# A sparse mixture's first products rotate through four banks late in the loop, with rows transposed three tiles ahead, gating four steps behind and outputs six behind

## What is computed

```python
logits = jnp.einsum('bsd,de->bse', x, Wg)
top_vals, top_idx = jax.lax.top_k(logits, TOP_K)          # 2 of 8
probs = jax.nn.softmax(top_vals, axis=-1)
for e in range(E):
    u = jnp.einsum('bsd,dh->bsh', x, W1[e])               # 128 -> 256
    v = jnp.einsum('bsd,dh->bsh', x, W2[e])
    h = u * jax.nn.sigmoid(u) * v
    y = jnp.einsum('bsh,hd->bsd', h, W3[e])               # 256 -> 128
    out = out + y * weights[..., e][..., None]
x = x + jnp.tanh(g_ffn[1]) * out
```

## Time and profile before

| | us |
|---|---|
| median of 3 runs | 926.17 |
| lowest, highest | 923.63, 931.97 |
| profiled execution, its own time | 930.39 |
| its span, first to last instruction | 928.6 |
| mean granted TensorE clock | 0.933 |

### The profile page before, as it was taken

One profiled execution on the slowest core, in us unless ns is written; L12 is line 12 of the kernel. 1 busy time (PEld: TensorE's weight loads), 2 busy tenths in 40 slices (PEclk: granted clock), 3 DMA queues, 4 the chain that ended last, 5 costly groups with the idle time before them and its releaser, 6 DMA issues. The chain is left out here.

```text
span 928.6 us, 26325 instructions
## 1 busy us (share of the span) xinstructions
PE 793.4 (85%) x8408; PEld 610.8 (66%) x8408; DVE 720.4 (78%) x3041; ACT 571.9 (62%) x1209; POOL 466.9 (50%) x504
## 2 busy tenths in 40 slices
PE   4999999999999599999998898865678888888870
PEld 2566666666666356677775676765577887888860
DVE  3989899889898769899999988644465666668864
ACT  3777777777776456887887766443334555555530
POOL 3653454445444011376676765646555554555550
PEclk9999999999999879989999989877779999999995
DMA  9001001000100200011111111311122322245628
GB/s 242 30 23 41 20 20 37 22 20 20 39 1 2 59 1 10 13 50 45 46 45 39 53 44 35 88 49 58 58 67 73 96 79 69 78 125 163 178 81 277
DMA packets 62211, 57.95 MB, mean 62 GB/s; under 512 B 10320, under 2 KB 52099, under 8 KB 62115
## 3 DMA queue, kind: packets, MB, share of 16 engines
q1 hardware_dynamic: 44547, 34.25, 13.2%
q0 software_dynamic: 8640, 17.84, 5.7%
q10 hardware_dynamic: 8928, 4.70, 1.8%
HBM read 32.74 MB, written 24.02 MB: 61 GB/s over the span
## 5 line engine op out<-in xcount | busy, mean ns | idle before, releaser
L1113 POOL DMA_INDIRECT contributions<-v_heads,d_token x142 | 136.6, 962 | 120.4 <-DVE v_heads L1301 76.2
L1741 PE MATMUL bc_bank<-d_xT,d_w 128*128 128x128 f32 x1136 | 161.9, 288 | 39.7 <-DVE b_hidden L1290 17.1
L1741 PEld LDWEIGHTS bc_bank<-d_xT,d_w 128*128 128x128 f32 x1136 | 145.7, 201 | 46.8 <-DVE d_xT L1285 35.1
L1105 POOL DMA_INDIRECT sorted_rows<-r_send,r_slots x128 | 126.8, 990 | 50.2 <-issue 34.6
L1510 ACT ACTIVATE b_hidden<-bc_bank 128x256 f32<-128x256 f32 x142 | 54.4, 383 | 154.4 <-PE bc_bank L1741 121.1
L1285 DVE COPY d_xT<-bc_bank 128x128 f32<-128x128 f32 x142 | 40.8, 287 | 94.3 <-PE bc_bank L1760 66.3
L432 POOL TENSOR_SCALAR a_k_heads<-a_kT,first 128x512 f32<-128x512 f32 x60 | 93.2, 1570 | 0.8 <-ACT a_kT L483 0.8
L1517 ACT COPY d_w<-w 128x512 f32 x142 | 86.9, 612 | 2.2
L507 ACT ACTIVATE a_probs<-a_scores 128x1024 f32<-128x1024 f32 x64 | 65.6, 1025 | 29.4 <-PE a_scores L607 29.3
L350 DVE TENSOR_REDUCE a_neg_max<-a_scores 128x16 f32<-128x1024 f32 x64 | 78.1, 1220 | 6.8 <-PE a_scores L597 5.3
L514 ACT COPY a_probsT<-a_probsT_bank 128x512 f32<-128x512 f32 x128 | 74.7, 584 | 11.7 <-PE a_probsT_bank L624 11.1
(11 more groups left out here) (215 smaller groups left out, 1884.8 us busy)
## 6 DMA issues: line engine op xcount, KB each, us to landing
d_rows<-sorted_rows SPq DMA_DIRECT2D x142, 65.0 KB
X<-in_x SPq DMA_DIRECT2D x16, 256.0 KB, 3.0
b_hidden<-contributions SPq DMA_DIRECT2D x8, 512.0 KB
b_weighted<-contributions SPq DMA_DIRECT2D x8, 512.0 KB
out_x<-X ACTq DMA_DIRECT2D x16, 256.0 KB
ctxT<-in_ctx_T SPq DMA_DIRECT2D x16, 192.0 KB, 2.9
c_ctxT<-in_ctx_T SPq DMA_DIRECT2D x16, 192.0 KB
contributions<-v_heads,d_token POOLq DMA_INDIRECT x142
```

What stands on the lines that cost most here:

```text
L1105: pool.indirect_dma_start(dispatch.rows, bass.IndirectOffsetOnAxis(ap=slots[n % 2][:, k, j:j + 1], axis=0), send[n % 2][k][:, j, :], None) ...
L1113: pool.indirect_dma_start(dispatch.contributions, bass.IndirectOffsetOnAxis(ap=token[:, t % KEEP:t % KEEP + 1], axis=0), shares[t % KEEP], ...
L1741: last = pe.matmul(uv[m % 2][:, bass.ts(i, P)], w12[m % 3][:, bass.ts(i, P)], xT[m % 4][:], start=True, stop=True)
```

## The change

It changes how far behind each other the parts of a tile run, and how many banks the first products use.

| | before | after |
|---|---|---|
| first products and Silu of tile m | step m+2 | step m+3 |
| gating of tile m | step m+2 | step m+4 |
| second products and share of tile w | step w+4 | step w+6 |
| banks of first products | bc_bank0, bc_bank1 | the same below tile 20, then bc_bank0, bc_bank1 and both halves of bc_pair in turn |
| first products wait for gating of | tile m-2 | tile m-2 below tile 22, then tile m-4 |
| Silu slots | 2 | 4 |

The tiles 22 and 23 are the first ones in bc_pair; they wait for the last attention work in it. The steps run to 147 instead of 145, since the outputs of the last tiles come six steps behind.

```diff
-    HIDDEN, OUT = 2, 4
+    HIDDEN, GATED, OUT, FOUR = 3, 4, 6, 20
...
-    silu = tails[0:2]
-    d_hidden = [b.rearrange("p (k n) -> p k n", k=KH) for b in tails[2:6]]
+    silu = tails[0:4]
+    d_hidden = [b.rearrange("p (k n) -> p k n", k=KH) for b in tails[4:8]]
...
-    uv, y_bank = bank[0:2], (bank[5], bank[2])
+    y_bank = bank[5], bank[2]
+
+    def uv(m):
+        return (bank[0][:], bank[1][:], pair[:, 0], pair[:, 1])[m % 2 if m < FOUR else m % 4]
...
-                m = t - HIDDEN
+                m = t - GATED
                 if 0 <= m < DTILES:
                     dve.wait_ge(silu_done, m + 1)
-                    dve.tensor_tensor(d_hidden[m % 4].rearrange("p k n -> p (k n)"), silu[m % 2],
-                                      uv[m % 2][:, KH * P:2 * KH * P], ALU.mult).then_inc(h_ready, 1)
+                    dve.tensor_tensor(d_hidden[m % 4].rearrange("p k n -> p (k n)"), silu[m % 4],
+                                      uv(m)[:, KH * P:2 * KH * P], ALU.mult).then_inc(h_ready, 1)
...
-                    if m >= 2:
-                        act.wait_ge(h_ready, m - 1)
-                    act.activation(silu[m % 2], uv[m % 2][:, 0:KH * P], ACT.Silu).then_inc(silu_done, 1)
+                    if m >= 4:
+                        act.wait_ge(h_ready, m - 3)
+                    act.activation(silu[m % 4], uv(m)[:, 0:KH * P], ACT.Silu).then_inc(silu_done, 1)
...
-                    if m >= 2:
-                        pe.wait_ge(h_ready, m - 1)
+                    if m < 2:
+                        pe.wait_ge(k_ready if m == 0 else weighted_ready[0], G)
+                    elif m == FOUR + 2:
+                        pe.wait_ge(xrT_ready, G)
+                    elif m == FOUR + 3:
+                        pe.wait_ge(x1_updated, G)
                     else:
-                        pe.wait_ge(k_ready if m == 0 else weighted_ready[0], G)
+                        pe.wait_ge(h_ready, m - 1 if m < FOUR + 2 else m - 3)
```

More of the change, by code:

```diff
@@ L1735, in sparse @@
                     pe.wait_ge(w12_ready, m + 1)
-                    if m >= 2:
-                        pe.wait_ge(h_ready, m - 1)
+                    if m < 2:
[4 more added lines that the diff above has]
+                        pe.wait_ge(x1_updated, G)
                     else:
-                        pe.wait_ge(k_ready if m == 0 else weighted_ready[0], G)
+                        pe.wait_ge(h_ready, m - 1 if m < FOUR + 2 else m - 3)
                     for i in range(2 * KH):
-                        last = pe.matmul(uv[m % 2][:, bass.ts(i, P)], w12[m % 3][:, bass.ts(i, P)], xT[m % 4][:], start=True, stop=True)
+                        last = pe.matmul(uv(m)[:, bass.ts(i, P)], w12[m % 3][:, bass.ts(i, P)], xT[m % 4][:], start=True, stop=True)
                     last.then_inc(hidden_mm, 1)
```

## The result

| | before | after |
|---|---|---|
| median, us | 929.07 (4 runs) | 947.37 (4 runs) |
| range | 923.63 to 932.4 | 944.92 to 955.14 |
| profiled execution, its span | 928.6 | 943.1 |
| mean granted clock | 0.933 | 0.933 |

The changed kernel takes 1.0225 of the time of before, 95% interval 1.0178 to 1.0271: it is 1.8 to 2.7% slower. 913 us was predicted, in a range of 897 to 932; the result lies above the range, and the change goes the other way.

What follows compares the result with a forecast made beforehand. It took TensorE and the vector engine, waiting for each other in a ring with late TensorE signals, as the bound. Terms -17.4 - 6.9 + 10 + 1 = -13.3 us turned 926.2 into 913 us, range 897 to 932.

Steps and rivals of the forecast that it cites:

- The ring, and its tolerances of 0.45 us before and 1.34 after: TensorE and vector engine wait for each other; a signal late by up to 0.45 us, then 1.34, costs nothing.
- At the mean wait of 0.9, nothing would be left: Steps 25 to 107: at TensorE's mean gating wait of about 0.9 us, the new tolerance leaves no loss.
- the choice of 1.58 us: Steps 25 to 107: step taken as 1.58 us, between 1.47 without waiting and 1.79 now; gain 17.4 us.
- The late stretch, -6.9 us: Steps 108 to 140: 1.64 us per step instead of 1.85, with a floor of 1.54; gain 6.9 us, ends 0 and 10.
- The start, +10 us (4 to 25): First 25 steps, two banks only: the ring becomes serial, 2.50 us per step instead of 1.45; costs 10 us.
- steps 6 to 11: Part of the start, mixed with TensorE's last attention work: six serial steps at 2.50 us, 15.0 instead of 12.97; +2.0.
- The scatter behind share 11: Part of the start: routing group 15's scatter on GpSimd comes 11.4 us behind step 14 instead of 7.4; +4.0.
- the steps of the two holds: Start, 637 to 654 and 664 to 681: TensorE gets one step less far (4.0 us), two shares fewer (2.5); +3.0.
- The tail, +1 us (0 to 2.5): End of the mixture: two steps more, with second products alone; costs 1 us.
- The second one: Rival: lags use up the new tolerance; steady step 1.75 us, early +13, tail +2, 936 us; chance 0.22.
- The first rival: Rival: signal lags don't grow; steps of 1.48 and 1.56 us, about 899 us in all; chance 0.15.
- The signs it named: Prediction wrong if steady step stays above 1.70 us or falls below 1.50, or step 25 comes under 3 or over 20 later.

Runs made afterwards that it cites:

- e9: Changed kernel with shares from tile 12 on written by SyncE's queue as whole tiles, row places left out; 901.2 us, 0.9683 of the kernel before, late signals in set.
- e14: Changed kernel with four short GpSimd copies behind each share's DMA from tile 12 on; 944.9 us, 1.0197 of the kernel before, in a set with late signals.
- e15: Kernel before with shares from tile 12 on written by SyncE as whole tiles, row places left out; 881.1 us, 0.9521 of before, late signals in set.
- e11: Changed kernel with gating three behind and outputs five behind; 931.2 us, 1.0038 of the kernel before, in a set with late signals.
- e6: Changed kernel, unchanged, run again in a set without late signals; 877.7 us, 1.0255 of the kernel before.
- e5: Kernel before, unchanged, run again for a trace in a set without late signals; 855.1 us.
- e12: Kernel of e9 with two GpSimd multiplications per share from tile 12 on in place of the DMAs; 907.3 us, 0.9786 of the kernel before.
- e13: Changed kernel with shares from tile 12 on written as whole tiles from GpSimd's own queue, row places left out; 906.4 us, 0.979 of the kernel before.
- e10: Changed kernel with two short GpSimd copies behind each share's DMA from tile 12 on; 941.3 us, 1.0146 of the kernel before, late signals in set.
- e16: Kernel before with three short GpSimd copies behind each share's DMA from tile 12 on; 894.7 us, 1.0402 of before, no late signals in set.
- e17: Changed kernel with three short GpSimd copies behind each share's DMA; 900.8 us, 1.0482 of the kernel before, no late signals in set.

## Why the prediction was wrong, point by point

**The ring, and its tolerances of 0.45 us before and 1.34 after: right, or nearly, where signals are late.** Before, a lag of 1.30 us makes a step of 2.30 instead of 1.45 (steps 57 to 59): 0.85 lost, as 0.45 of tolerance has it. After, a lag of 2.82 makes one of 3.15 (steps 65 to 68): 1.70 lost, where 1.34 of tolerance gives 1.48. The waits for gating vanished, as told. One wait was not in the list: the transpose needs the copy made two vector steps back, and with lags of 2.8 us it is where TensorE stops first (12.3 us, and 5.6 at the second products).

**"At the mean wait of 0.9, nothing would be left", and the choice of 1.58 us: the step that failed.** It took the lag of a signal as a given size that slack can cover: -17.4 us, of which the stretch shows -1.6. By the traces the loop itself makes the lag. A held signal lets TensorE run ahead as far as its banks allow; on release the vector engine makes up the steps 1.1 us apart; their shares reach GpSimd as one bunch; the bunch is issued back to back, and the next signals come only behind it. With more slack the bunches are of four instead of three, and the vector engine sees the end of a step 2.8 us late instead of mostly 1.3 to 2.1. e9, e14 and e15 show that there are no lags in the steady part without GpSimd's dense indirect DMAs; that the length of a bunch sets the lag is read from the cycles of before, after and e11, and no run sets it by itself. Steps 25 to 56 did profit (1.61 us per step, 1.81 before, 6.4 us in all), until the loop fell into the longer cycle; from 57 to 107 a step is 1.87 instead of 1.78 and 4.8 of them are lost again. The fear was in the text ("a faster loop drives GpSimd ..."), but was priced at a third of the way.

**The late stretch, -6.9 us: the same failure.** 61.1 instead of 61.0 us. Its floor of 1.54 us per step was too high as well: without late signals the 33 steps take 47.9 us in e6, 1.45 each.

**The start, +10 us (4 to 25): the mechanism right, the size low.** +13.1 in the profiled pair, +22.1 where nothing is late. By places, in the pair: steps 6 to 11 take 22.2 us instead of 13.0, +9.3 where +2.0 was taken. The sum priced them at 2.50 each, but three of them, from 626.64 to 638.60, run at a granted clock of 0.50, and a serial step at that level is 3.99 us (4.0 stands in the prediction, for the holds alone). The scatter behind share 11 starts 13.8 us behind step 14 instead of 7.4: +6.4 for +4.0. Against it, the steps of the two holds (12 and 13, and 20 to 22) take 0.8 us less together, where +3.0 was taken. Without late signals (e6) all but one of the steps from 10 to 23 take 2.56 us each, where most in the kernel before (e5) take 1.45 to 1.58.

**The tail, +1 us (0 to 2.5): low.** +4.8 in the profiled pair, +3.4 in e6 against e5 (from step 141 to the end 36.7 and 33.3 us). Among the last second products there are waits of 2.12 and 0.28 us for the share two back, and GpSimd's last DMA starts 13.8 us behind step 141 instead of 8.8: six tiles are still under way there instead of four.

**The rivals.** The second one, lags that use up the tolerance, is what happened in the first comparison: a steady step of 1.77 where 1.70 was said to decide, 936 us by its sum and 947 measured. Of the 11 us between, 3.1 are steady steps and 2.8 the tail, and the start is as it had it; the rest lies outside the profiled pair, whose spans differ by 14.5 us while the medians differ by 18.3. It had a chance of 0.22, and slower as a whole 0.17. The first rival ("the signal lags don't grow", 899 us) did not come true: they grew here and in e11. And no rival spoke of runs in which no signal is late at all, though the argument hung on lags that were seen in one execution.

**The signs it named.** The steady step stayed above 1.70, which was said to mean that it is wrong. Step 25 came 11.2 us later, within 3 to 20.

## What to carry to other kernels

Before slack is bought for a wait, ask whether the wait is caused by something that the loop feeds: here the delay was longer behind longer bursts, and slack made the bursts longer. A ring that crosses two engines is counted in steps between producer and consumer; moving one stage back a step while the number of buffers stays the same can make it serial, and here the first 25 steps paid 13 to 22 us for steps behind them that gained 1.5 at most. And where a stall has no instruction that explains it, run the same kernel again, on another chip if there is one, before spending on it.

## What the runs showed of the hardware

TensorE's completion signals can come late by much more than any work in the trace accounts for: 0.04 us behind the modelled end where nothing holds them, but up to 3.3 us in the steady part and up to 15.4 us in the first stretch (the Silu at 653.93 after 14.65 us of waiting, for products that began at 637.36) while GpSimd issues indirect DMAs of 0.96 us 1.26 us apart. Arithmetic on GpSimd doesn't do it (e12), whole tiles from its queue, 0.54 us with pauses of 0.9, don't either (e13), and pauses of 0.7 to 0.9 us between indirect DMAs remove it (e14), while 0.47 leaves it (e10). No run has whole tiles from GpSimd's queue without such pauses, so whether the indirect form matters, or only that GpSimd issues back to back, stays open. TensorE's following matmuls start on time meanwhile (766.21 and 767.66). That agrees with the Trainium skill, "SBUF — State Buffer", who interferes with whom (PE and ACT never wait on anyone), as far as execution goes; the page doesn't speak of signals, and whether the products or only the signal are late can't be told here, because the end shown is an estimate, as the Trainium skill, "Perfetto Trace Analysis", says of the Tensor Engine instruction.

It does not always happen. The kernel before took 927 to 930 us in three sets and 857 to 859 in four, with one and the same program, its runs within a set agreeing to about 1%; and in e5 the 149 indirect DMAs from 639.7 to the last, never more than 0.32 us of pause between them, held nothing. It doesn't go by the chip's number on record: one number appears with lags (e9 to e11) and without (e16, e17). What decides it stays open.
